# Scores from stacked high and low parts through device memory, and exponents formed on VectorE

## What is computed

```
q, k, v = h_in @ wq, h_in @ wk, h_in @ wv          # 8 heads of 32, 32 and 64
logfg = log_sigmoid(f_pre); Fcum = cumsum(logfg)
Dmat = Fcum[..., :, None] - Fcum[..., None, :] + i_pre[..., None, :]
m = max(Dmat, -1) over t <= s;  Smat = exp(Dmat - m)      # zero for t > s
C = (q @ k.T / sqrt(32)) * Smat
n = maximum(abs(sum(C)), exp(-m));  h = (C / n) @ v
x1 = x + (sigmoid(o_pre) * rmsnorm_of_heads(h)) @ w_out
out = x1 + (silu(h2 @ w_gate) * (h2 @ w_up)) @ w_down     # FF = 2048
    + ghost MLP of the same form, INTER = 1376
```

## Time and profile before

| | |
|---|---|
| median of 3 runs | 2474.1 us |
| the profiled execution, its own time | 2471.92 us |
| its span | 2470.1 us |
| TensorE matmul busy | 2416.0 us (98%) |
| VectorE busy | 1253.8 us (51%) |
| ScalarE busy | 914.9 us (37%) |
| GpSimd busy | 610.8 us (25%) |
| DMA | 508.34 MB, 206 GB/s |

### The profile page before, as it was taken

One profiled execution on the slowest core, in us unless ns is written; L12 is line 12 of the kernel. 1 busy time (PEld: TensorE's weight loads), 2 busy tenths in 40 slices (PEclk: granted clock), 3 DMA queues, 4 the chain that ended last, 5 costly groups with the idle time before them and its releaser, 6 DMA issues. The chain is left out here.

```text
span 2470.1 us, 33080 instructions
## 1 busy us (share of the span) xinstructions
PE 2416.0 (98%) x11376; PEld 1947.6 (79%) x11376; DVE 1253.8 (51%) x2205; ACT 914.9 (37%) x1683; POOL 610.8 (25%) x499
## 2 busy tenths in 40 slices
PE   7999999999999999999999999999999999999998
PEld 5677787787787778778777877888888888888887
DVE  6776536765773675577367557743222222222222
ACT  5433245355454535545443544554111111111111
POOL 2346523221321322232132223222111111111111
PEclk9999999999999999999999999999999999999999
DMA  5055554473464448356444825676867867867865
GB/s 210 1 199 207 216 226 140 167 275 127 152 213 182 154 166 281 107 172 208 167 162 165 293 102 174 208 265 223 279 237 273 282 241 260 296 241 255 287 221 198
DMA packets 115513, 508.34 MB, mean 206 GB/s; under 512 B 11120, under 2 KB 11120, under 8 KB 80144
## 3 DMA queue, kind: packets, MB, share of 16 engines
q1 hardware_dynamic: 110016, 496.46, 57.2%
q10 hardware_dynamic: 5328, 9.70, 1.3%
HBM read 417.39 MB, written 87.69 MB: 204 GB/s over the span
## 5 line engine op out<-in xcount | busy, mean ns | idle before, releaser
L747 PE MATMUL up_bank<-act_hi,gud 128*128 128x512 f32 x1728 | 591.8, 403 | 0.0
L747 PE MATMUL gate_bank<-act_hi,gud 128*128 128x512 f32 x1728 | 574.7, 393 | 2.7 <-DVE th L1587 2.7
L2073 POOL TENSOR_TENSOR hidden_lo<-hm,hidden_hi 128x512 fp32r<-128x512 f32 x216 | 281.9, 1305 | 1136.3 <-ACT hidden_hi L1131 1136.3
L947 PE MATMUL acc<-gud,hidden_hi 128*128 128x512 f32 x1728 | 436.2, 394 | 0.9 <-ACT hidden_hi L1131 0.9
L1587 DVE SCALAR_TENSOR_TENSOR th<-th,gate_bank 128x512 f32<-128x512 f32 x216 | 147.9, 685 | 514.3 <-ACT th L1126 514.2
L1131 ACT ACTIVATE hidden_hi<-hm 128x512 fp32r<-128x512 f32 x216 | 135.9, 629 | 692.6 <-PE acc L950 681.2
L747 PEld LDWEIGHTS up_bank<-act_hi,gud 128*128 128x128 f32 x1728 | 324.6, 188 | 81.0 <-issue 13.5
L747 PEld LDWEIGHTS gate_bank<-act_hi,gud 128*128 128x128 f32 x1728 | 324.3, 188 | 75.1 <-DVE th L1587 4.6
L947 PEld LDWEIGHTS acc<-gud,hidden_hi 128*128 128x128 f32 x1728 | 319.5, 188 | 68.1 <-issue 4.2
L747 PE MATMUL up_bank<-act_lo,gud 128*128 128x512 f32 x864 | 337.7, 391 | 0.0
L747 PE MATMUL gate_bank<-act_lo,gud 128*128 128x512 f32 x864 | 336.7, 390 | 0.0
(11 more groups left out here) (326 smaller groups left out, 2973.0 us busy)
## 6 DMA issues: line engine op xcount, KB each, us to landing
gud<-mlp_parts SPq DMA_DIRECT2D x112, 1024.0 KB, 5.1
gud<-ghost_parts SPq DMA_DIRECT2D x88, 1024.0 KB, 5.9
gud<-mlp_parts SPq DMA_DIRECT2D x112, 512.0 KB, 3.9
gud<-ghost_parts SPq DMA_DIRECT2D x88, 512.0 KB, 4.6
ghost_parts<-look_w SPq DMA_DIRECT2D x35, 512.0 KB, 3.8
mlp_parts<-gud SPq DMA_DIRECT2D x16, 1024.0 KB, 3.9
vo_w_hi<-vo_parts SPq DMA_DIRECT2D x13, 1024.0 KB, 7.1
vo_w_lo<-vo_parts SPq DMA_DIRECT2D x13, 1024.0 KB, 9.9
```

The source lines that it names most:

```text
L747: mm = pe.matmul(dst, l[a], r[c], start=first and k == 0 and n == 0, stop=last and k == len(lhs) - 1 and n == 2)
L947: pe.matmul(ACC[i][:], HH[0][:, toks(i)], W3[:, z, 2, n, :], start=t == 0 and n == 0, stop=False)
L2073: pool.tensor_tensor(HH[1][:], hm[:], HH[0][:].bitcast(f32), ALU.subtract).then_inc(of.low.sem, 1)
```

## The change

The exponents' matmul is gone. ACT stores the running maxima (`store_max`, 16 KB) to device memory and loads them back to all 128 partitions (`load_max`, 512 KB for each 128 tokens, four for each half-stage). DVE forms m[s] - a[t] and the mask in four instructions of 128 columns for each unit, one for each head, with a as a column; Exp gets a scale of -1. The rows that `factors` transposes grow from 72 to 104, since a goes with them. POOL's `mx_`, and DVE's and ACT's rows for `AL` and `mhl`, are gone.

The scores, in all half-stages but FIRST, are four float32r matmuls for each unit, one for each head, of 96 rows by 128 by 128: the rows are stacks of high and low parts of 32 channels (high, high, low against high, low, high). ACT copies `gate_bank` rounded into `stack`, DVE forms the low part (`qkT_lo`), ACT stores both to device memory (`store_qk`, two DMAs of 256 KB for each 128 tokens), and SP loads each unit's stack back in another layout (`load_qk`, six DMAs of 64 KB). `stack` has two slots, so ACT waits in `qkT_(2)` and `qkT_(3)` until the stores of slots 0 and 1 have landed. PE's `q_k_T(i)` now waits for DVE's low part of i - 1 as well. `qbd_` is left only in FIRST. In FIRST's loop `q_k_T` of SECOND stands behind `unit_2`.

```diff
@@ PE
             def q_k_T(at, i):
                 wait(pe, act_qk, at, i, "k")
                 if i:
-                    wait(pe, act_qkT, at, i - 1, "k")
+                    wait(pe, act_qkT, at, i - 1, "done")
+                    if not here(at, FIRST):
+                        wait(pe, vec_qkT, at, i - 1, "lo")
...
-                pe.matmul(pick(at, u, A, ACC[0])[:], AL[:, toks(j)], MX[:, g * HG:(g + 1) * HG, :], start=True, stop=True)\
-                    .then_inc(pe_unit.sem, 1)
...
+                pe.wait_ge(ld_qk[u % 2], stack_loaded(at, u))
+                if u:
                     wait(pe, vec_unit, at, u - 1, "update")
-                pe.matmul(pick(at, u, B, ACC[1])[:], qkT_of(at)[:, 1, g, toks(j)], pick(at, u, qbd, qbd2)[:, :, :], start=True, stop=True)\
-                    .then_inc(pe_unit.sem, 1)
+                for h in range(HG):
+                    mm = pe.matmul(B[:, toks(h)], stack[0:3 * DQ, u % 2, 1, toks(h)], stack[0:3 * DQ, u % 2, 0, toks(h)],
+                                   start=True, stop=True)
+                mm.then_inc(pe_unit.sem, 1)
@@ ACT
             def exps(at):
+
                 wait(act, vec_rows, at, 0, "bound")
-                for r in range(0, RW, 32):
+                for r in range(0, 96, 32):
                     act.activation(rwe[r:r + H, :], rows(at)[3][r:r + H, :], ACT.Exp).then_inc(act_gates.sem, 1)
+                act.activation(rwe[96:96 + H, :], rows(at)[2], ACT.Copy).then_inc(act_gates.sem, 1)
+
+            def store_max(at):
+                wait(act, vec_rows, at, 0, "max")
+                act.dma_start(max_rows.rearrange("j h n -> h j n"), mx[:, 1:].rearrange("h (j n) -> h j n", j=NB))\
+                    .then_inc(st_max, 16)
+
+            def load_max(at, j):
+                if j == 0:
+                    act.wait_ge(st_max, at[0] * (HALVES * 16) + (at[1] * 16 + 16))
+                elif j >= 2:
+                    wait(act, vec_unit, at, 2 * j - 3, "masked")
+                act.dma_start(mq[:, j % 2, :, :], max_rows[j].unsqueeze(0).to_broadcast([P, H, P]))\
+                    .then_inc(ld_max[j % 2], 16)
...
+                if i >= 2:
+                    act.wait_ge(st_qk[i % 2], stacked(at, i // 2))
+                act.activation(stack[:, i % 2, 0, :], GB[:], ACT.Copy).then_inc(act_qkT.sem, 1)
+                act.activation(qT[:, :, i * P:(i + 1) * P], both[:, 0], ACT.Copy).then_inc(act_qkT.sem, 1)
+
+            def store_qk(at, i):
+
+                if here(at, FIRST):
+                    return
+                wait(act, vec_qkT, at, i, "lo")
+                for part in range(2):
+                    src = stack[:, i % 2, part, :].bitcast(f32).rearrange("p (z n) -> p z n", z=2)
+                    act.dma_start(qk_parts[part::2, i].rearrange("z p n -> p z n"), src).then_inc(st_qk[i % 2], 16)
@@ SP
+            def load_qk(at, u):
+
+                i, g = u // G, u % G
+                if u < 2:
+                    sp.wait_ge(st_qk[u], stacked(at, NB // 2))
+                else:
+                    wait(sp, pe_unit, at, u - 2, "scores")
+                for r, parts in enumerate((slice(0, 3, 2), slice(0, 4, 3), slice(1, 3))):
+                    dst = stack[r * DQ:(r + 1) * DQ, u % 2, :, :].bitcast(f32).rearrange("d z (h n) -> d z h n", h=HG)
+                    src = qk_parts[parts, i, :, g * P:(g + 1) * P].rearrange("z (h d) n -> d z h n", h=HG)
+                    for z in range(2):
+                        sp.dma_start(dst[:, z], src[:, z]).then_inc(ld_qk[u % 2], 16)
@@ DVE
+            def qkT_lo(at, i):
+                wait(dve, act_qkT, at, i, "done")
+                dve.tensor_tensor(stack[:, i % 2, 1, :], GB[:], stack[:, i % 2, 0, :].bitcast(f32), ALU.subtract)\
+                    .then_inc(vec_qkT.sem, 1)
...
+                    qkT_lo(at, 0)
+                    qkT_lo(at, 1)
                     dve.wait_ge(st_mlp[1 - at[1]], at[0] * 16)
                 gate_sum(at)
+                if not here(at, FIRST):
+                    qkT_lo(at, 2)
                 gate_maxima(at)
+                if not here(at, FIRST):
+                    qkT_lo(at, 3)
                 gate_factors(at)
...
             def unit_1(at, u):
-                wait(dve, pe_unit, at, u, "exponents")
+                j, g = u // G, u % G
+                dve.wait_ge(ld_max[j % 2], max_loaded(at, j))
...
+                c = j * RW + 96 + g * HG
+                for h in range(HG):
+                    ins = dve.scalar_tensor_tensor(pick(at, u, ar, ar2)[:, h, :], mq[:, j % 2, g * HG + h, :], rn[:, c + h:c + h + 1],
+                                                   maskd[:], ALU.subtract, ALU.max)
+                ins.then_inc(vec_unit.sem, 1)
```

More of the change, by code:

```diff
@@ L317, in program @@
         st_vo = sem("st_vo")
+        st_qk = [sem(f"st_qk{i}") for i in range(2)]
+        ld_qk = [sem(f"ld_qk{i}") for i in range(2)]
         ld_idx = [sem(f"ld_idx{i}") for i in range(2)]
@@ L323, in program @@
         look_vec = sem("look_vec")
+        st_max = sem("st_max")
+        ld_max = [sem(f"ld_max{i}") for i in range(2)]
         st_x1 = sem("st_x1")
@@ L606, in _ @@
             store_xt(1, XH[1])
+            for u in range(2):
+                load_qk(SECOND, u)
             wait(sp, vec_norm, FIRST, NB - 1, "gated")
@@ L624, in tiles @@
                 for t in range(NM):
+                    if not here(at, TAIL) and 1 <= t < UNITS - 1:
+                        load_qk(at, t + 1)
                     if here(at, SECOND):
@@ L651, in tiles @@
                             store_xt(b * HALVES + half, XH[half])
+                            for u in range(2):
+                                load_qk(at, u)
                     if looks(at):
@@ L832, in unit_2 @@
                     wait(pe, vec_unit, at, u - 2, "state")
-                pe.matmul(pick(at, u, B, ACC[1])[:, 0:HG * VS], qkT_of(at)[:, 0, g, toks(j)], kv[:, g, :, :], start=True, stop=True)
+                pe.matmul(pick(at, u, B, ACC[1])[:, 0:HG * VS], qT_of(at)[:, g, toks(j)], kv[:, g, :, :], start=True, stop=True)
                 for h in range(HG):
@@ L856, in ho_T @@
                 else:
-                    wait(pe, act_qkT, SECOND, NB - 1, "k")
+                    wait(pe, act_qkT, SECOND, NB - 1, "done")
+                    wait(pe, vec_qkT, SECOND, NB - 1, "lo")
                 f = hn[:, :, :].rearrange("p h d -> p (h d)")
@@ L907, in gate @@
                 if t == 0 and stage:
-                    wait(pe, act_qkT, stage, NB - 1, "k")
+                    wait(pe, act_qkT, stage, NB - 1, "done")
+                    wait(pe, vec_qkT, stage, NB - 1, "lo")
                 else:
@@ L1309, in front @@
                 gate_logs(at)
+                store_qk(at, 0)
                 qk(at, 2)
@@ L1312, in front @@
                 qk(at, 3)
+                store_qk(at, 1)
                 gate_rows(at)
@@ L1315, in front @@
                 v(at, 0)
+                store_qk(at, 2)
                 qkT_(at, 3)
-                a_high(at)
+                store_qk(at, 3)
                 v(at, 1)
+                store_max(at)
                 v(at, 2)
                 exps(at)
+                for j in range(2):
+                    load_max(at, j)
                 if here(at, FIRST):
@@ L1335, in qbd_ @@
                 j, g = u // G, u % G
[L1336 to L1343 removed]
+                if u >= 2:
+                    wait(act, pe_unit, at, u - 2, "scores")
+                wait(act, act_qkT, at, j, "part")
                 for h in range(HG):
[L1345 removed]
+                    act.activation(pick(at, u, qbd, qbd2)[:, h, :], qkT_first[:, 0, g, j * P:(j + 1) * P], ACT.Copy,
                                    scale=bdm[:, h:h + 1]).then_inc(act_qbd.sem, 1)
@@ L1383, in units_first @@
                         v(at, u - 6)
+                    if u in (4, 5, 6, 7):
+                        store_qk(at, u - 4)
                 ho_T(FIRST, 2)
@@ L1415, in h2_T @@
                                    ACT.Copy).then_inc(act_h2T.sem, 1)
-                if stage:
-                    qbd_(at, 0)
                 for t in range(NM):
@@ L2124, in units_first @@
                     x1_root(at, i)
-                mx_(SECOND, 0)
                 for part in (0, 1):
@@ L2133, in tiles @@
                 done = 0
-                if stage and not here(at, SECOND):
-                    mx_(at, 0)
                 for t in range(NM):
```

139 lines of the change are left out of this document (47 added, 92 removed).

## The result

| | before | after |
|---|---|---|
| median | 2475.56 us (2473.74 to 2477.68, 4 runs) | 2510.56 us (2509.97 to 2513.18, 4 runs) |
| the profiled execution, its span | 2471.92, 2470.1 us | 2513.18, 2511.4 us |
| DMA moved | 508.34 MB | 561.98 MB |

The ratio is 1.0143, 95% interval 1.0126 to 1.0161. The forecast was 2471.2 with a range from 2439 to 2496, and the measured time lies above it.

What follows compares the result with a forecast made beforehand. TensorE, busy 98% of the span, was taken as the bound; -14.5 - 24.6 + 0.8 + 3 + 32.4 = -2.9 us gave 2469.0 us profiled, 2471.2 as the median, no change that can be told, range 2439 to 2496.

Steps and rivals of the forecast that it cites:

- Exponents on PE: On TensorE, 64 exponent products of 0.23 us each disappear: 14.5 us less.
- factors: On TensorE, transposes of 104 columns instead of 72 take 0.1 us more, eight times: 0.8 us more.
- Scores: On TensorE, four float32r products take 0.43 us a unit against 0.87, in 56 units: 24.6 us less.
- rival of four streams: Narrow float32r score products stream four times, 0.87 us a unit, so nothing is saved: 2496 us, slower; chance 0.15.
- The new wait: In six loop fronts ACT waits for block 0's store, stalling PE 4.0 us plus 1.4 of clock: 32.4 us more.
- 1.4 us of work lost: After each front's stall PE's granted clock drops, costing 1.0 + 0.4 us, read from an earlier 2.85 us stop.
- case of a landing of 9.7 or more: Block 0's store lands after 9.7 us or more, not 8.4; the stall alone makes the kernel over 5 us slower.
- rival of a store that lands at once: In the fronts ACT's store lands in 5.0 us, PE waits 0.6 each, no clock loss: 2442 us; chance 0.30.
- In the tiles this is hidden: VectorE's exponents, 1.4 us against 0.69 a unit, cost PE nothing in the tiles, since VectorE is busy half the time.
- FIRST, +3: In FIRST's units VectorE has less cover; of 5.5 us extra work, 3 reach PE, between 0 and 8.
- What costs nothing: Removing `qbd_` and `mx_` gains nothing; loads of maxima and stacks and SP's extra DMA issues do not delay PE.
- sum of -2.9: All terms on PE together: 2.9 us less, 2469.0 us profiled and 2471.2 as the median.

Runs made afterwards that it cites:

- psum_in: Changed kernel with the exponents' first operand read from PSUM, except in unit 0 and FIRST's units (wrong exponents, for times only): 2492.5 us, ratio 1.0076.

## Why the prediction was wrong

- **Exponents on PE, -14.5, and factors, +0.8**: right (-14.8 and +0.9).
- **Scores, -24.6**: right (-23.5 on PE, and 21.6 for as many products again). The rival of four streams, from 0.143 us a product on, is out at 0.096.
- **The new wait, +32.4**: the mechanism, its place, its six occurrences and the chain behind it (1.65 us, forecast 1.8) were right; two sizes were too small. The landing of both DMAs was taken as 8.4 us and was 12.0 from the first issue, past the upper end of 7.2 + 3.4 = 10.6 even, so the stall was 6.0 and not 4.0. The clock, "1.4 us of work lost" behind a gap of 2.85 us, was 2.2 behind a gap of 6; the 1.4 was itself read short, since the stretch of 755 to 756 with a clock of 0.69 belongs to it and makes it 1.7. Together the fronts cost 51.6: 19.2 short. The case of a landing of 9.7 or more is what happened. The rival of a store that lands at once is out in this kernel: the store took 10.8 us in the median with SP's megabytes in flight, and 6.7 with 2 MB fewer, where the rival had 5.0. The rule of turns between queues in the Trainium skill, page "DMA: Bandwidth & Descriptors", section "Queues, rings and completion order", was weighed in the prediction as making it likely; these landings do not show whether turns were taken, only that they did not make the store fast.
- **"In the tiles this is hidden"**: the step that failed. VectorE's busy share of half and its 62.7 us of waiting for exponents were read as cover in every unit. The cost of the four instructions was taken as 1.4 us everywhere; it is 1.13, or 2.5 to 2.6 in units 4 and 6 of a pass, where GpSimd's instructions hold them, and there PE waits. Forecast 0, measured +18.8, and `psum_in`, which takes the hold away, gives 18 back. The row that would have warned is the earlier trace rows: the old instruction's source is a PSUM bank, the new one's are both in SBUF.
- **FIRST, +3**: about 3.4, right in size, though one of its terms does not follow: 1.4 - 0.69 is 0.71 a unit and 5.7 in eight, not "8 x 0.6 = 4.9". The start (+2.6 in this trace) was not looked at: a constant's fill of 1.0 us on GpSimd was removed, and the next one, of 1.9, moved up beside VectorE's normalization.
- **What costs nothing**: loads of the stacks and maxima, weight tiles: right, PE waits for none of them.

From the sum of -2.9 to 41.3 there are 44.2 us: 19.2 in the fronts, 18.8 in the tiles and about 6 elsewhere, where the start, the gaps around 250 to 285 us, the loop's branch and the scores are 7.0 and SECOND's tiles take 0.9 off. Either miss alone would have left the time inside the range, at 2490; the two together make 2509.

## What to carry to other kernels

When a copy to device memory frees its source only on landing, price the landing under the transfers that other queues have in flight at that moment, and put an idle PE's lower clock on top; here a second place to stage was worth 49 us and a later store on another queue 45. When work moves from TensorE to VectorE, ask tile by tile what VectorE has to do there, and from which memory each operand comes: an instruction that used to read PSUM can be held for the length of a GpSimd instruction once both inputs are in SBUF. Two halves of a change that each lean on the same slack must be measured together as well as apart.

## What the runs showed of the hardware that was not expected

- A VectorE instruction of 128 columns with two tensors in SBUF took 0.34 us with GpSimd quiet and 1.38 us where a GpSimd instruction of 1.33 us had begun 0.10 us before; with one of the two in PSUM it took 0.34 us beside the same GpSimd instruction.
- A store of two times 256 KB from ACT's queue took 10.8 us in the median from issue to landing with SP's transfers in flight, the last two of them 1 MB each that took 12.0 and 13.8 us, 6.7 us without these two, and 2.9 us with the engines 16% busy.
- A gap of PE of 6 us was followed by some 5 us at 1.2 GHz and cost 2.2 us beyond itself. One of 2.85 us was followed by 3.4 us at that clock (0.69 granted in 755 to 756, then), which is 1.7 us of work. Gaps of equal length need not cost the same: one of 2.89 us before 281.94 in the kernel before left the clock at 1.00, and one of 2.89 us before 280.59 in the kernel after was followed by 0.54 in 281 to 283 and 0.60 in 283 to 285.
